# A folded query product, a residual added by accumulation, and a transposition moved behind the projections

## The reference

```
nodes = {-1: inputs}
for c in range(6):
    nsrc = min(c + 1, 5); snode = c - nsrc
    in_q, in_k, in_v = (c - 1, snode, snode + nsrc // 2)
    q = ew[c, 0] * (nodes[in_q] @ We[eq] + be[eq])
    k = ew[c, 1] * (nodes[in_k] @ We[ek] + be[ek])
    v = ew[c, 2] * (nodes[in_v] @ We[ev] + be[ev])
    o = _mha(q, k, v, Wq[c], Wk[c], Wv[c], Wo[c])     # 8 heads of 16
    nodes[c] = act_w[c] * o + q
out = nodes[5]
```

## Time and profile before

| | before |
|---|---|
| median of 3 runs | 2217.35 us (2217.06 to 2220.44) |
| the profiled execution: its time, its span | 2223.95 us, 2221.9 us |
| PE busy | 2039.9 us (92%) |
| DVE busy | 1737.5 us (78%) |
| ACT busy | 1486.8 us (67%) |
| POOL busy | 341.7 us (15%) |
| mean granted TensorE clock | 0.949 |
| chain that ended last | PE 81%, DVE 13%, issue 4% |

### The profile page before, as it was taken

The page is one execution under the profiler, slowest core; times in us unless marked ns, Lnnn a source line. Parts: engine busy times, 40 slices in busy tenths (PEclk is TensorE's granted clock), DMA queues, the critical chain, the costliest instruction groups (busy, mean ns, idle before and its releaser), DMA issues.

```text
span 2221.9 us, 32029 instructions
## 1 busy us (share of the span) xinstructions
PE 2039.9 (92%) x10812; PEld 846.9 (38%) x10812; DVE 1737.5 (78%) x3501; ACT 1486.8 (67%) x2004; POOL 341.7 (15%) x385
## 2 busy tenths in 40 slices
PE   5748886999999999999999999999999999999995
PEld 2224443333333333444444444444444444443332
DVE  5856887788787877888888888888878888888884
ACT  4743453566666677777777777777777777776664
POOL 1101332000000011111111111111111111113223
PEclk9977786799999999999999999999999999999998
DMA  3001104233333355566566656556666566665630
GB/s 103 19 24 54 56 33 86 43 66 75 63 75 67 82 104 107 117 109 109 109 109 109 108 109 109 108 110 109 109 110 108 108 109 109 109 108 101 98 58 25
DMA packets 137197, 195.63 MB, mean 88 GB/s; under 512 B 20152, under 2 KB 55632, under 8 KB 137040
## 3 DMA queue, kind: packets, MB, share of 16 engines
q1 hardware_dynamic: 137040, 193.63, 45.5%
HBM read 75.45 MB, written 23.73 MB: 45 GB/s over the span
## 4 chain that ended last, share of the span: by engine, by line
PE 81%; DVE 13%; issue 4%; ACT 1%; POOL 1%; DMA 1%; DVEq 0%; POOLq 0%; SPq 0%; ACTq 0%
PE bank_s L1031 27%; PE bank_o L1069 22%; PE bank_x L1054 6%; DVE nm L1386 5%; PE bank_m L1082 3%; PE bank_x L1017 3%; PE bank_x L996 3%; PE bank_x L1004 2%; PE bank_m L1102 2%; PE bank_x L983 2%; PE bank_x L1128 2%; PE bank_s L934 1%; DVE big L1275 1%; PE bank_m L1092 1%; PE bank_m L1041 1%
## 5 line engine op out<-in xcount | busy, mean ns | idle before, releaser
L1386 DVE TENSOR_REDUCE nm<-bank_s 128x1 f32<-128x512 f32 x2048 | 1336.2, 685 | 342.3 <-PE bank_s L1031 341.4
L821 ACT ACTIVATE big<-bank_x 128x1024 f32<-128x1024 f32 x1024 | 1048.0, 1024 | 486.5 <-PE bank_x L1054 458.9
L1031 PE MATMUL bank_s<-kst,qst 62*128 62x512 f32 x2048 | 837.5, 469 | 53.1 <-DVE nm L1386 52.5
L1054 PE MATMUL bank_x<-qst,kst 64*128 64x512 f32 x2048 | 750.0, 447 | 1.6 <-ACT big L821 1.6
L1031 PEld LDWEIGHTS bank_s<-kst,qst 62*128 62x128 f32 x2048 | 358.9, 187 | 693.3 <-DVE nm L1386 609.4
L1069 PE MATMUL bank_o<-big,at 128*32 128x512 f32 x4096 | 556.4, 616 | 2.2 <-ACT big L821 2.0
L1054 PEld LDWEIGHTS bank_x<-qst,kst 64*128 64x128 f32 x2048 | 304.3, 187 | 10.2 <-issue 6.0
L605 POOL CAST at<-at 128x512 fp32r<-128x512 f32 x112 | 68.2, 609 | 1273.3 <-ACT at L752 1035.8
L607 POOL TENSOR_TENSOR at<-at 128x512 fp32r<-128x512 f32 x112 | 143.3, 1280 | 10.0
L1069 PEld LDWEIGHTS bank_o<-big,at 128*32 128x32 f32 x4096 | 81.2, 108 | 153.1 <-issue 149.2
L829 ACT ACTIVATE big<-bank_x,big 128x128 f32<-128x128 f32 x256 | 68.7, 376 | 27.3 <-issue 11.6
(11 more groups left out here) (154 smaller groups left out, 1511.4 us busy)
## 6 DMA issues: line engine op xcount, KB each, us to landing
at<-nodes_d SPq DMA_DIRECT2D x144, 256.0 KB, 5.9
kst<-at SPq DMA_DIRECT2D x288, 128.0 KB
qst<-at SPq DMA_DIRECT2D x288, 128.0 KB
nodes_d<-big SPq DMA_DIRECT2D x48, 256.0 KB, 3.1
at<-w_d SPq DMA_DIRECT2D x48, 193.0 KB, 5.8
at<-x2T_d SPq DMA_DIRECT2D x32, 256.0 KB, 4.4
kst<-at SPq DMA_DIRECT2D x128, 64.0 KB
qst<-at SPq DMA_DIRECT2D x128, 64.0 KB
```

Of the source, the lines that this page charges most:

```text
L821: act.activation(PT[:, kp, h, :, :], ring.take()[0].rearrange("p (c n) -> p c n", c=2), ACT.Exp, scale=x.c.scale).then_inc(S["c_ex"], 1)
L1031: pe.matmul(bank_s[:, n % 2, :], qst[rows, x.r, h, t * P:(t + 1) * P], kst[rows, x.r, h, :], start=True, stop=True).then_inc(S["c_s_ps"], 1)
L1054: mm = pe.matmul(sec(to, j), kst[rows, x.r, h, kc_ * P:(kc_ + 1) * P], qst[rows, x.r, h, :], start=True, stop=True)
L1386: dve.tensor_reduce(nm[:, k, at_n:at_n + 1], bank_s[:, n % 2, :], AX.X, ALU.max, negate=True).then_inc(S["c_red"], 1)
```

## The change

- **Query product folded.** A sixth kind of weight product, We[eq] times Wq, is formed ahead of the units (with `WeQT`, the transposed We[eq], loaded too) and scaled by ew. The query projection is one product of the node's input: `proj_q` and `ev_qT` are gone. `ev_qh` adds the folded bias.
- **Residual by accumulation.** `out_proj` issues two products into the same place of `bank_m`: the scaled We[eq] times the node's input, then the old one. VectorE's `node_out` becomes ScalarE's `ev_wo` in step (1, 0), which adds one bias that has both parts.
- The node's input is kept for that in six buffers `nq` instead of being part of `st_qk`; the four `q_sb` are gone. Loads have the same bytes in total: `load_qk` takes 258 columns of `w_d` instead of 386, `load_o` 257 instead of 129.
- **Projections moved.** `proj_kh` of a graph unit stands in step (1, 2) instead of (1, 6), `proj_qh` in (1, 6) instead of (1, 7).
- **Maxima's transposition moved.** `maxima` and `ev_m` stand in steps (0, 2) and (1, 2), behind the value or key projection and its eviction, instead of (0, 1) and (1, 1).

```diff
@@ load_qk
-                when((S["c_kh_ps"], x.u - 1), *[(S["c_qh_ps"], x.un - 1)] * x.c.node)
+                when((S["c_kf_ev"], x.u - 1), *[(S["c_qf_ev"], x.un - 1), (S["c_wo_ps"], x.un - NQ + 1)] * x.c.node)
...
+            def ev_wo(x):
...
+                need(act, S["c_wo_ps"], x.un + 1)
...
+                act.activation(no_sb, bank_m[:, :], ACT.Identity, bias=st_o[x.half][:, 2 * P:2 * P + 1]).then_inc(S["c_wo_ev"], 1)
@@ body of ScalarE
                         if i == 1:
                             ev_pv(*((last, 1) if k == 0 else (x, 0)))
-                        if i == 1:
-                            ev_m(*led_group(c, q, r, k))
                         if k == 0:
                             if i == 2:
                                 ev_v(at_(c, q, r + 1))
+                                ev_m(*led_group(c, q, r, k))
                             if i == 6:
                                 ev_cT(last)
                         else:
+                            if i == 0:
+                                ev_wo(last)
                             if i == 1:
                                 ev_final(last)
                             if i == 2:
-                                ev_qT(ahead)
-                                ev_kh(only(ahead, False))
+                                ev_kh(ahead)
+                                ev_m(*led_group(c, q, r, k))
                             if i == 6:
-                                ev_kh(only(ahead, True))
+                                ev_qh(ahead)
                             if i == 7:
-                                ev_qh(ahead)
                                 ev_x3T(last)
@@ weight products
+                pe.matmul(q_product(c), wv(c, "WeQT"), wv(c, "WqP"), start=True, stop=True)
+                pe.matmul(b_product(c, 0), wv(c, "WqP"), vec(c, 0), start=True, stop=True)
@@ out_proj
-                pe.matmul(bank_m[:, :], st_o[x.half][:, 0:P], ctxT, start=True, stop=True).then_inc(S["c_wo_ps"], 1)
+                pe.matmul(bank_m[:, :], st_o[x.half][:, P:2 * P], nq[x.un % NQ], start=True, stop=False)
+                pe.matmul(bank_m[:, :], st_o[x.half][:, 0:P], ctxT, start=False, stop=True).then_inc(S["c_wo_ps"], 1)
@@ body of TensorE
-                        if i == 1:
-                            maxima(*led_group(c, q, r, k))
...
                             if i == 2:
                                 value(at_(c, q, r + 1))
+                                maxima(*led_group(c, q, r, k))
...
                             if i == 2:
-                                proj_q(ahead)
-                                proj_kh(only(ahead, False))
+                                proj_kh(ahead)
+                                maxima(*led_group(c, q, r, k))
                             if i == 6:
-                                proj_kh(only(ahead, True))
+                                proj_qh(ahead)
                             if i == 7:
-                                proj_qh(ahead)
                                 turn_x3(last)
@@ body of VectorE
-                        if (k, i) == (1, 0):
-                            node_out(last)
```

More of the change, by code:

```diff
@@ L734, in _ @@
             ring = Slots()
-            def ev_qT(x):
-                x = only(x, True)
-                if x is None:
-                    return
-                need(act, S["c_qT_ps"], x.un + 1)
-                need(act, S["c_wo_ev"], x.un - RING + 1)
-                act.activation(q_sb[x.r], ring.take()[0][:, 0:L], ACT.Identity, bias=st_qk[x.half][:, 3 * P:3 * P + 1]).then_inc(S["c_q_ev"], 1)
             def ev_kh(x, src=None):
@@ L751, in ev_kh @@
                     need(act, S["c_sp"], 2 * x.u - 1)
[L752 removed]
+                    act.activation(kf, src, ACT.Identity, bias=st_qk[x.half][:, 2 * P + 1:WA]).then_inc(S["c_kf_ev"], 1)
                 else:
@@ L762, in ev_qh @@
                 need(act, S["c_sp"], 2 * x.u)
-                act.activation(qf, ring.take()[0][:, 0:L], ACT.Copy).then_inc(S["c_qf_ev"], 1)
+                act.activation(qf, ring.take()[0][:, 0:L], ACT.Identity, bias=st_qk[x.half][:, 2 * P:2 * P + 1]).then_inc(S["c_qf_ev"], 1)
             def ev_v(x, src=None):
@@ L894, in _ @@
             ev_cT(end)
+            ev_wo(end)
             ev_final(end)
@@ L973, in slot @@
                 return to
-            def proj_q(x):
-                x = only(x, True)
-                if x is None:
-                    return
-                t = st_qk[x.half]
-                need(pe, S[f"c_qk{x.half}"], loaded(x, kn.loads_qk))
-                to = slot(S["c_q_ev"], x.un + 1)
-                pe.matmul(to[:, 0:L], t[:, 0:P], t[:, WA:WA + L], start=True, stop=True).then_inc(S["c_qT_ps"], 1)
             def proj_kh(x, to=None):
@@ L1001, in proj_qh @@
                     return
-                need(pe, S["c_q_ev"], x.un + 1)
+                need(pe, S[f"c_qk{x.half}"], loaded(x, kn.loads_qk))
                 to = slot(S["c_qf_ev"], x.un + 1)
-                pe.matmul(to[:, 0:L], st_qk[x.half][:, P:2 * P], q_sb[x.r], start=True, stop=True).then_inc(S["c_qh_ps"], 1)
+                pe.matmul(to[:, 0:L], st_qk[x.half][:, 0:P], nq[x.un % NQ], start=True, stop=True).then_inc(S["c_qh_ps"], 1)
             def value(x, to=None):
@@ L1375, in _ @@
             dve.wait_ge(S["p_mm"], 2)
-            dve.tensor_copy(po_sb[:, :, WN - 1], bank_o[:, 0:NODES]).then_inc(S["p_ev"], 1)
+            for c in range(NODES):
+                i = dve.scalar_tensor_tensor(po_sb[:, c, WN - 1:WN], vec(c, 0), vec(c, 3), bank_o[:, c:c + 1], ALU.mult, ALU.add)
+            i.then_inc(S["p_ev"], 1)
             def reduce(x, k, n):
@@ L1608, in _ @@
             final_norm(last, 3)
-            node_out(end)
             for step in range(4):
```

61 lines of the change are left out of this document (30 added, 31 removed).

## The result

| | before | after |
|---|---|---|
| median of 4 runs | 2218.89 us (2217.06 to 2222.44) | **2245.15 us** (2241.22 to 2248.22) |
| profiled execution: span | 2221.9 us | 2246.3 us |
| mean granted TensorE clock | 0.949 | 0.951 |
| one graph unit in the long stretch | 27.70 us | 28.235 us |

What follows compares the result with a forecast made beforehand. The prediction took TensorE to be the pace, with VectorE the pace in light steps. Its terms, 49.4 - 18.7 + 2.4 + 1.5 = +34.6 us, on 2217.35 gave 2252.0 us, range 2238 to 2272.

Steps and rivals of the forecast that it cites:

- Matrix work does not fall; it moves: TensorE's total stays: `proj_q` goes, an equal residual product comes, 53.9 and 53.2 us busy, moving work into step (0, 7).
- Step (0, 7), +1.03: The residual product behind the output projection lies wholly on the path, 1.03 us a unit: 48 x 1.03 = +49.4 us.
- Steps (1, 7) and (0, 0), -0.39: Without the query projection, 2.69 us shrinks only to 2.30, held by VectorE's two maxima: 48 x 0.39 = -18.7 us.
- The maxima's move, +0.05: Maxima evicted later, `turn` of step (1, 3) up to 0.3 us late, mostly hidden: 48 x 0.05 = +2.4 us.
- `node_out` off VectorE, 0: VectorE loses 0.74 us, but nothing waits for it; output products of (1, 0) and (1, 1) cover it: 0.
- `ev_wo` for `ev_qT`, 0: ScalarE swaps evictions of the same kind, 0 in total; in (1, 0) the next exponential is some 0.2 us later.
- The front, +1.5: Before the units: a scaling reads TensorE's bank and the last bias costs six small operations: about +1.5 us, bounds 0 and 4.
- the clock falls: Rival: emptied (1, 7) lowers TensorE's clock, about 1.55 us in half of the 48 units, +37 us more, 2289; chance 0.05.
- VectorE's busy time, -36 us: Sign to look for in the profile: VectorE's busy time falls by 36 us, TensorE's stays about unchanged but for its gaps.
- the vector engine is the pace in fact: Rival, faster: maxima of (1, 7) do not hold (0, 0), whole 1.37 us comes back against 1.03, 2202.5 us; chance 0.08.
- Gain and cost: Rival: `node_out` does delay maxima, so its 0.66 us slot comes back, 31.7 us, leaving +3, 2220 us; chance 0.06.
- The turn in full: Rival: `turn` waits wholly for the maxima's eviction, 0.45 us a unit instead of 0.05, +19.2 more, 2271 us; chance 0.08.

## Why the prediction was right, and where not

The forecast was 34.6 us more, measured were 26.3 in the medians and 24.4 between the profiled spans. Side and range were right, and so was the mechanism of the steady unit. That the total came out so near is in part luck, since the two stretches that the sum did not price, the first attention (-10.0) and the last seven periods (5.7 more than seven steady units), partly cancel. By its own steps:

- **Matrix work does not fall; it moves.** Right, and the root of the result. Without the residual product the unit is 0.865 us shorter.
- **Step (0, 7), +1.03: mis-sized.** It is +0.86. The prediction took a product's length from one that stands among score products. Two 128-row products in a row need 0.93 and 0.96 us instead of 1.03 each. 48 x 0.17 = 8 us too much.
- **Steps (1, 7) and (0, 0), -0.39.** Exact: the outputs stand at 2.30 us, released as computed from the two maxima of 1.29 us. The runs with a product more (+0.27 for 1.06) and with short maxima (-0.33) show the cause from both sides.
- **The maxima's move, +0.05.** The sum is right (+0.06 by the steps), its parts are not. Named was only the late `turn` in (1, 3): that came, 0.98 us behind the step's start, and is hidden, since (1, 3) and (1, 4) together take 3.30 us as before (3.29). But VectorE's divisions come late too, and with them its maxima, and (1, 5) and (0, 5) pay 0.17 and 0.10. On the other side the transposition is cheaper beside a projection (0.11) than behind outputs (0.21), which the prediction held to be equal.
- **`node_out` off VectorE, 0: half right.** With step (1, 1) at its old length it is 0: steps (1, 0) to (1, 2) of the run with the maxima back last as long as before, with `node_out` gone. With the transposition moved out of (1, 1) that cover is gone, and `node_out` costs 2.01 - 1.83 = 0.18 us. So the change needed this part to make its other move cheap. The prediction costed each alone, and by costing the removal at nothing, since the output products of (1, 0) and (1, 1) cover it, it left out that the change itself takes 0.21 us of the cover away.
- **`ev_wo` for `ev_qT`, 0.** No wait for either shows in the step table.
- **The front, +1.5.** The scaling stretch grew by 1.4. The front as a whole differs by more than that from one run to another.
- **Not in the sum: the first attention, -10.0 us.** The move of the transposition is in the loop of all 64 units. Units in which the clock stays up are 0.22 and 0.33 us shorter in turn (26.26 to 26.04, 28.84 to 28.51), together some 4 us. The rest goes with the granted clock. In the unit of the earlier trace rows it is half for the outputs behind the two light steps (1.77 us). In neighbouring windows of 4 us from 424 to 880 us its mean is 0.974 before and 0.989 after, and 456 x 0.015 = 6.8 us is what that can give at most, since a wait for another engine is not part of it. With the transposition back in its old place the mean is 0.977; in the ten runs with it in step 2 it is 0.981 to 0.996. Of these, the changed kernel and the run with the emptied step (1, 2), whose edit touches graph units alone, differ by 3.3 us and by 0.989 against 0.996, so some 3 us of this term can be chance. In stretches of 200 us, before (the third column from the end is the clock),

```profile
400.00:600.00 200.00, 186.26 (x1036) 74.53 (x1036) 158.98 (x317) 133.12 (x156) 16.86 (x20) 0.94 0.31 64
600.00:800.00 200.00, 187.27 (x1079) 75.43 (x1077) 162.24 (x323) 137.96 (x164) 18.69 (x22) 0.97 0.34 77
```

after,

```profile
400.00:600.00 200.00, 185.30 (x1053) 74.53 (x1052) 161.37 (x322) 135.17 (x158) 16.89 (x20) 0.95 0.31 64
600.00:800.00 200.00, 185.15 (x1107) 75.81 (x1103) 167.22 (x338) 141.74 (x168) 18.78 (x22) 1.00 0.37 82
```

and in the changed kernel with the transposition back in its old place

```profile
400.00:600.00 200.00, 186.24 (x1022) 74.86 (x1021) 159.28 (x316) 130.59 (x153) 16.87 (x20) 0.93 0.30 62
600.00:800.00 200.00, 186.44 (x1074) 75.26 (x1074) 162.80 (x326) 137.56 (x162) 18.25 (x22) 0.97 0.36 80
```

  That the place of the transposition did it is shown by the runs with it in either place; how it keeps the clock up five steps later stays open. The range had reserved "a little" for it.
- **Not in the sum: the last seven periods, +9.5 us.** There the final norm is on VectorE as well, and a part of it, placed in step (1, 5), makes the maxima late up to the step that the change emptied. In one of these periods after:

```profile
2030.00:2034.00 4.00, 3.35 (x14) 1.20 (x10) 4.00 (x10) 2.74 (x3) 2.73 (x3) 1.00 0.00 0
2034.00:2038.00 4.00, 3.50 (x14) 1.17 (x16) 2.41 (x4) 1.02 (x1) 3.46 (x4) 0.62 0.16 53
```

  VectorE is busy for the full 4 us, TensorE has 14 instructions, and then its clock falls to 0.62, between 1.2 and 2.4 GHz. This is the rival "the clock falls", in a few periods instead of in half of the units. The same stretch of a period before, with a projection in (1, 7), keeps 1.00:

```profile
2048.00:2052.00 4.00, 3.72 (x15) 1.54 (x18) 3.88 (x7) 2.99 (x5) 3.84 (x5) 1.00 0.00 0
2052.00:2056.00 4.00, 4.00 (x32) 1.68 (x25) 3.24 (x12) 3.03 (x5) 1.83 (x3) 1.00 0.67 119
```

  Period by period, with the mean granted clock:

  | period | 1 | 2 | 3 | 4 | 5 | 6 | 7 |
  |---|---|---|---|---|---|---|---|
  | before, us | 30.75 | 30.87 | 30.90 | 30.90 | 32.31 | 26.07 | 18.70 |
  | clock | 1.00 | 1.00 | 1.00 | 1.00 | 0.89 | 1.00 | 1.00 |
  | after, us | 33.11 | 32.80 | 31.65 | 31.67 | 32.11 | 27.08 | 21.56 |
  | clock | 0.95 | 0.95 | 1.00 | 1.00 | 0.95 | 1.00 | 0.84 |

  Of the 9.5 us, seven times the steady 0.535 are 3.7. The falls of the clock in the first two periods are 1.45 + 1.14 = 2.6 against the 31.66 of the next two. The other 3 or so lie in longer waits and, in the last period, in the lower clock, and were not parted. The kernel before has a fall of its own, in the fifth. In the first four periods the clock falls in four of the five kernels with (1, 7) emptied, one to three times each; the fifth is the one with the short maxima. It does not fall there in any of the seven with a product in (1, 7). With one profile of each this points to the emptied step together with VectorE's load. The Trainium skill (TensorE: Matmul & The Clock Gate, A second HAM failure mode) describes matmul groups with small idle times between them whose clock goes up and down; the trace agrees for these units (0.62) and not for the steady ones (1.00), which have small idle times too (30 us in 1000).
- **VectorE's busy time, -36 us.** It fell by 18.7 on the page, although the group of `node_out` with its 35.7 us is gone and no other group grew by more than 1. The page counts an engine's overlapping rows once. Row by row the durations fell by 36.8 us, as forecast, but neighbouring rows of VectorE overlap by 208.7 us in all and no longer by 226.8: 7.8 of these 18.1 us were overlaps of `node_out` with maxima, 6.9 overlaps of the divisions' reciprocals with maxima.

From the sum to the spans: 34.6, less 7.4 for 48 steady units at 0.535 (the residual above all), less 10.0 for the first attention, and then 1.0 for the front, 5.7 for the last seven periods beyond 0.535 each and 0.5 for the last unit: 24.4.

The rivals: with the whole projection back, as in the rival "the vector engine is the pace in fact", (1, 7) + (0, 0) would have lasted 3.69 - 1.37 = 2.32 us; they last 3.30. Gain and cost would have cancelled if the removal of `node_out` gave 0.66 us back; it gives 0 where the rest of its surroundings is unchanged. The turn in full would have cost 0.45 us a unit; the late divisions cost 0.27 in both halves together. The clock fell, but only in the last periods.

## What to carry to other kernels

Count instructions before believing that a fold saves work: here a product folded away came back as the residual, since its result had two uses, and moving it from a step where VectorE was the pace to one where TensorE was cost 0.47 us a unit. Where two engines take turns as the pace from step to step, price every change by the step from which it leaves and the step into which it goes, and price the parts together where one takes away the cover of another. And look for the small instruction beside the large ones: the fastest kernel kept the old algorithm, put a 128-column transposition ahead of a projection, formed the node's output in two halves and put one projection into a free bank. By the medians the first of these edits gave 18 of its 28 us.

## What the chip showed that was not expected

- The time that a product takes on TensorE goes with its neighbours. A 128x512 fp32 product (two instructions) takes 1.03 to 1.06 us to the next start among score products, which use 62 or 64 rows, but 0.93 and 0.96 next to another 128-row product. Behind the transposition it took 0.96 in two runs and 1.03 in two others; what decides between them was not found.
- The 128-column transposition of the maxima costs 0.21 us behind output products, 0.11 behind a projection, and 0.02 ahead of one where it starts 0.66 us into its step and the projection takes 0.96.
- In the two stretches around the steady units small changes of a step moved the granted clock: up in the first attention (mean 0.974 to 0.989 from 424 to 880 us), down in the last seven periods (0.983 to 0.959). In the 40 steady units between them it stayed at 1.00 in both kernels.
